# Order of VectorE's work in a graph kernel's projection stage: products and scores two steps back, the dense rows' inverse and shift among the spread rows

## The reference

```python
Q = jnp.einsum('nf,hfd->hnd', x, qw)
K = jnp.einsum('nf,hfd->hnd', x, kw)
Qr = Q[:, row]
alpha = jnp.einsum('hed,hed->he', Qr, K[:, col]) / scale
seg_max = jax.vmap(lambda a: jax.ops.segment_max(a, col, num_segments=n))(alpha)
a = jnp.exp(alpha - seg_max[:, col])
...
h = (h - mu) / jnp.sqrt(var + EPS) * ln_gamma + ln_beta
h = h * jax.nn.sigmoid(h)
return h @ out_w + out_b
```

## Time and profile before

| | us |
|---|---|
| three timed runs, median (lowest to highest) | 3175.5 (3161.36 to 3175.55) |
| the profiled execution | 3167.55 |
| its span, from first to last instruction | 3165.4 |
| busy in the span: DVE | 2318.9 (73%) |
| busy: ACT | 2112.9 (67%) |
| busy: POOL | 1909.8 (60%) |
| busy: PE | 1851.7 (58%) |
| mean share of the DMA queues q1 and q0 | 50.8% and 17.0% |

### The profile page before, as it was taken

How to read it: one execution, slowest core, us unless ns; L and a number is a source line. 1 busy time by engine, 2 the same in 40 slices (tenths; PEclk the granted TensorE clock), 3 DMA queues, 4 the chain that set the end, 5 groups by cost and what they waited for, 6 DMA issues and landing times.

```text
span 3165.4 us, 54101 instructions
## 1 busy us (share of the span) xinstructions
PE 1851.7 (58%) x9516; PEld 1390.9 (44%) x9516; DVE 2318.9 (73%) x8807; ACT 2112.9 (67%) x5382; POOL 1909.8 (60%) x1839
## 2 busy tenths in 40 slices
PE   4666666444555453777777666657656666344442
PEld 4566565333333332445554333346545555233332
DVE  7888878766666664777886666658868888788883
ACT  4888887434444333878887788845547777499995
POOL 6777775788888885333332755457757555045554
PEclk9777877677777776989898898889987777655555
DMA  5889987333333335999998899968867777344441
GB/s 185 298 291 299 303 294 249 70 62 64 61 60 61 61 54 144 336 340 331 337 353 303 306 322 322 323 198 257 264 202 264 254 254 254 119 131 135 126 133 53
DMA packets 325460, 670.59 MB, mean 212 GB/s; under 512 B 56604, under 2 KB 116127, under 8 KB 325396
## 3 DMA queue, kind: packets, MB, share of 16 engines
q1 hardware_dynamic: 244980, 554.40, 50.8%
q0 software_dynamic: 80416, 115.57, 17.0%
HBM read 346.98 MB, written 326.96 MB: 213 GB/s over the span
## 4 chain that ended last, share of the span: by engine, by line
DVE 17%; ACT 14%; issue 10%; DMA 9%; PE 7%; DVEq 2%; POOL 1%; ACTq 1%; SPq 0%; POOLq 0%
ACT node_out L1145 8%; DMA node_in<-y_nodes 4%; DVE acc L1512 3%; DMA node_in<-x_table 3%; PE ps L982 2%; DMA acc_dump<-acc 2%; ACT new_rows L1145 2%; DVE n_stats L1459 2%; DVE e_stats L1459 2%; PE ps L993 1%; DVE node_in L1763 1%; DVE pre L1865 1%; DVE pre L1932 1%; DVE a_stats L1459 1%; ACT gate L1321 1%
## 5 line engine op out<-in xcount | busy, mean ns | idle before, releaser
L1145 ACT ACTIVATE node_out<-node_in,n_shift,n_root 128x128 f32<-128x128 f32 (+1 forms) x1176 | 468.0, 482 | 125.1 <-DVE n_shift L1476 124.5
L702 POOL DMA_INDIRECT sums<-gat_sums,dst_safe_i x200 | 189.4, 947 | 306.0 <-DVE pre L1763 240.6
L767 POOL DMA_INDIRECT gat_sums<-sums,add_idx x200 | 328.9, 1644 | 68.0 <-issue 60.0
L819 POOL DMA_INDIRECT out_dram<-new_rows,out_index x200 | 200.2, 1001 | 251.1 <-ACT new_rows L1145 200.1
L1459 DVE BATCH_NORM_STATS2 n_stats<-node_in 128x6 f32<-128x256 f32 (+1 forms) x784 | 279.3, 419 | 75.1 <-DMA node_in<-y_nodes 61.8
L710 POOL DMA_INDIRECT src_rows<-x_table,row_i x208 | 204.5, 983 | 151.0 <-issue 52.3
L710 POOL DMA_INDIRECT sums<-x_table,row_i x192 | 189.7, 988 | 121.7 <-issue 47.2
L702 POOL DMA_INDIRECT own_rows<-x_table,row_i x200 | 195.9, 980 | 67.1 <-issue 55.5
L702 POOL DMA_INDIRECT src_rows<-in_x_dram,src_i x200 | 193.9, 970 | 69.4 <-issue 60.1
L710 POOL DMA_INDIRECT own_rows<-in_x_dram,dst_safe_i x200 | 195.2, 976 | 61.0 <-issue 59.8
L1154 ACT ACTIVATE t_a<-ps 128x512 f32<-128x512 f32 (+1 forms) x202 | 118.6, 587 | 164.6 <-PE ps L862 164.3
(11 more groups left out here) (346 smaller groups left out, 6594.1 us busy)
## 6 DMA issues: line engine op xcount, KB each, us to landing
own_rows<-x_table SPq DMA_DIRECT2D x300, 256.0 KB, 3.0
x_table<-node_out SPq DMA_DIRECT2D x144, 512.0 KB
acc_dump<-acc SPq DMA_DIRECT2D x200, 264.0 KB
node_in<-x_table SPq DMA_DIRECT2D x96, 512.0 KB
x_table<-new_rows SPq DMA_DIRECT2D x150, 256.0 KB
gat_sums<-node_x2t SPq DMA_DIRECT2D x49, 528.0 KB, 5.9
node_sums<-gat_sums SPq DMA_DIRECT2D x48, 528.0 KB
node_in<-in_x_dram SPq DMA_DIRECT2D x48, 512.0 KB
```

Of the source, the lines that this page charges most:

```text
L702: g_.indirect_dma_start(out=to[:, g.b, j, 0:width], out_offset=None, in_=tab, in_offset=bass.IndirectOffsetOnAxis(ap=indices(j), axis=0)). ...
L767: g_.indirect_dma_start(out=gat_sums[:, :], out_offset=bass.IndirectOffsetOnAxis(ap=add_idx[:, g.b, j:j + 1], axis=0), in_=sums[:, g.b, j, ...
L819: g_.indirect_dma_start(out=out[:, :], out_offset=bass.IndirectOffsetOnAxis(ap=at_tile(out_index, g, j), axis=0), in_=new_rows[:, g.b, j, ...
L1145: last = sc.activation(to[0:pn, g.b, j, :], rows[0:pn, g.b, j, 0:F], ACT.Identity, bias=NORM[k][2][0:pn, g.b, j:j + 1], scale=root[0:pn, j ...
```

## The change

In this stage's call of `pipeline` on DVE, products and score sums go from a lag of one step to two and stand between and behind the last spread rows. The inverse and the shift, so far one function between the second and the third spread row, are two functions now, one behind the first and one behind the second spread row. The addition of the constant row and the statistics of the dense block, so far ahead of the products, come last in the step.

```diff
                 v.tensor_tensor(node_in[0:pn, g.b, :, :], node_in[0:pn, g.b, :, :],
                                 local3_bc[0:pn, None, :].to_broadcast([pn, DJ, F]), ALU.add).then_inc(D["n_pre"].sem, 1)
+
+            def nodes_x3_moments(g):
+                pn = dense_p(g)
                 wait_done(dve, D["n_pre"], g)
                 wait_free(dve, D["n_row"], g)
                 moments((D, "n", g, node_in, pn, DJ))
 
-            pipeline(dve, DENSE_FULL, edges(spread[0], spread[1]) + [nodes(1, shifts(D, "n"))] + edges(spread[2], spread[3])
-                     + [nodes(0, nodes_x3_more)] + edges((1, products), (1, score_sums)))
+            def node_inverses(g):
+                at = NORM["n"][1][0:dense_p(g), g.b, :]
+                wait_done(dve, D["n_rt"], g)
+                v.reciprocal(at, at).then_inc(D["n_rc"].sem, 1)
+
+            def node_shifts(g):
+                pn = dense_p(g)
+                wait_done(dve, D["n_rc"], g)
+                shift_of(D, "n", g, pn, DJ, NORM["n"][1][0:pn, g.b, :])
+
+            pipeline(dve, DENSE_FULL, edges(spread[0]) + [nodes(1, node_inverses)] + edges(spread[1]) + [nodes(1, node_shifts)]
+                     + edges(spread[2], (2, products), spread[3], (2, score_sums)) + [nodes(0, nodes_x3_more), nodes(0, nodes_x3_moments)])
             dve.wait_ge(L["score"].sem, L["score"].at(STEPS))
```

## The result

The changed kernel took 3128.69 us, the median of 4 runs (3123.94 to 3132.63), beside 3174.49 us for the kernel before, the median of 4 runs (3161.36 to 3175.55). The ratio is 0.9864, with a 95% interval of 0.9835 to 0.9894: 45.8 us less. The prediction was 3125 us, in a range of 3104 to 3155.

What follows compares the result with a forecast made beforehand. A ring of waits between DVE and ACT bound the 7.22 us step; afterwards DVE's queue would, at 6.25 us. Saving 43 us in the loop plus 3 outside, 46, gave 3121.5 to 3129.5, so 3125 us, range 3104 to 3155.

Steps and rivals of the forecast that it cites:

- ring through `gate`: DVE and ACT before the change: node_out, copies, products, sums, spread rows, inverse, shift, node_out, 7.23 us round.
- DVE's queue, 6.03 us: DVE's instructions in one step, start to start, sum to 6.03 us; with the branch about 6.2, the largest bound.
- four terms that had no row of their own: Gaps in DVE's sum chosen between two ends: spread row to products, products to spread row, spread row to sums, variance to spread row.
- The branch, 0.15 to 0.18 us a step: DVE's loop branch, once in two steps: half of 0.36 us of bare register work between products and sums.
- Dependent spread rows: On DVE a dependent spread row starts after 0.50 us, an independent instruction after 0.27; two bare pairs a step before.
- ACT's ring, 5.98 us: From node_out 5.00 us to the next root, then inverse, spread row, shift and node_out: 5.98 us a step.
- Rival 4: On DVE, sums and products hide all register steps; ACT binds at 5.9 to 6.0 us, saving 54 to 60; chance 0.08.
- The loads' ring: Dense block loads over two steps: 7.55 us plus L, issue to landing; at most 6.05 a step with L 4.56.
- Rival 1: Dense block loads bind: landing in 5.3 to 6.1 us, steps of 6.4 to 6.8, 19 to 38 saved; chance 0.22.
- Rivals 2 and 3: DVE's inverse waits for ACT's root, 14 us slower, chance 0.04; register steps fill DVE, 0 to 15 saved, chance 0.08.
- The signs: Stage profile: products every 6.0 to 6.4 us, no `gate` wait, shorter `n_shift` wait, inverse within 0.3, DVE above 0.9.
- The sum: Stage saving: 0.97 us in each of 44 loop steps, 43 us, plus 3 us in written-out steps, 46 us.

Runs made afterwards that it cites:

- e2: Kernel before with inverse and shift set between spread rows, products and sums last at a lag of one step; 3155.56 us, ratio 0.9961.
- e1: Kernel before with its order kept and only products and score sums put back to a lag of two steps; 3151.73 us, ratio 0.9944.
- e3: Changed kernel with the dense sums ahead of products and score sums, lag two and mixed order kept; 3151.49 us, ratio 0.993 to the kernel before.
- e8: Changed kernel with the second spread row directly behind the first, ahead of inverse and shift; 3127.7 us in one run, mean step 6.56 us.
- e4: Changed kernel with inverse and shift both behind the first spread row, the other spread rows set apart by products and sums; 3124.53 us, ratio 0.9854.
- e7: Changed kernel storing only one row of eight of each finished dense block; 3125.5 us in one run, step 6.33 us.
- e6: Changed kernel with dense sums ahead of products and one row of eight of each finished dense block stored; 3136.77 us in one run.

## Why the prediction was right

*The rings.* The prediction read the step of before as a ring through `gate`. `e2` leaves that ring closed with inverse and shift in their new places, and stays at 7.0 us; the wait is there, and the ring's legs add up to 6.98. `e1` opens it and leaves the order, and the step falls to 6.9, nearly all of it DVE's queue with its gaps. The third part is needed too: with lag and mixed order but the dense sums ahead of the products (`e3`) the step is still 6.89. The prediction named this place in the change and gave it no term.

*DVE's queue, 6.03 us.* Measured 6.07 to 6.08 in the step without a branch. Of the four terms that had no row of their own, spread row to products was taken as 0.35 and is 0.28, products to spread row 0.60 and is 0.61, spread row to sums 0.35 and is 0.26, and variance to spread row 0.30 and is 0.46. That these errors cancel is luck; the 0.04 to 0.05 that are left come from inverse and shift to the spread rows behind them, 0.23 each where 0.21 was taken.

*The branch, 0.15 to 0.18 us a step.* This is the term that was mis-sized, and it was read at the wrong place. The prediction took it from products to sums, 1.11 us, but that is a row of the step without a branch. The branch stood between sums and spread row and lay bare for 0.26 us a pass, 0.13 a step, so the term came near its size by luck. In the changed kernel the two kinds of step are 0.49 us apart, 0.24 a step: 0.40 a pass at the branch, which now stands behind a variance of 0.17 us instead of sums of 0.69 and lies bare, and 0.07 between the last spread row and the sums, whose reason is open. The regular step is 6.32 us where 6.25 was forecast; 0.07 us over 44 steps are 3 us.

*Dependent spread rows.* 0.23 us for each pair set apart, and `e8` puts it back for one pair: 0.22. The prediction set against this the sentence of the Trainium skill's page "VectorE: DVE Perf Modes", section "The DRAIN you can't avoid", that the next operation does not start until the pipe is empty. The same section goes on that a next operation that is not held starts earlier, which the prediction left out; the traces agree with that: an independent instruction starts 0.27 us after a spread row of 0.35 us, one that waits for the row's semaphore after 0.50.

*ACT's ring, 5.98 us.* Measured 6.04: 5.01 to the root and 1.03 from the root to `node_out`. It lies just beneath DVE's queue; `e4` shortens it and gains nothing, so ACT's ring does not bind. Rival 4 did not come, since the register work is not hidden.

*The loads' ring.* Its form was right, 7.55 + L for two steps; with 4.4 us for L it is 12.0, and by the rows after up to 12.5. It was just short of binding. The prediction's last leg left out the branch, which lies between the addition and `node_out` of every second step: 4.75 us there and 4.34 in the other, where 4.18 was added up. That the ring would bind if products and sums stood between the addition and `node_out` was not said, and is what `e3` cost. Rival 1 itself came only in single steps, worth about 3 us by `e7`. Of the rule in the Trainium skill's page "DMA: Bandwidth & Descriptors", section "Latency and other measured facts", that the access time of HBM grows with load, little is seen in these loads: a median of 4.17 us at 196 GB/s and 4.24 at 270 (`e6`, `e3`), 4.14 in the kernel before and 4.37 in the changed kernel at 292 GB/s. What makes single `own_rows` loads take 6.5 us is not settled; the long steps that they made went with the stores' traffic, in one run.

*Rivals 2 and 3.* Past the first two steps, where it waited 4.16 and 1.55 us, the inverse waited no microsecond for a root in the changed kernel, and the step fell. Neither was seen.

*The signs.* The wait for `gate` is gone and ACT's wait for `n_shift` is 1.1 us, as said. Two signs missed: DVE's busy share is 0.89 from 2460 to 2560 us where above 0.9 was expected, and in the step with the branch the inverse starts 0.58 us after the root's end instead of within 0.3. Half of the regular steps, those of 6.56 us, lie outside the 6.0 to 6.4 that was named; their mean does not.

*The sum.* 46 us were predicted for the stage, and between the two profiled executions it is 40.6 us shorter: 3 us are missing by the regular step, 3 by the late loads. The medians of the whole kernel stand 45.8 us apart. That this meets the 46 so closely is luck: the runs of the kernel before lie 14 us apart and those of the changed kernel 9.

## What to carry to other kernels

Write out every ring that a step takes part in, those over two steps too, with each leg from a row, and compare their sums with the longest queue. After a change the next ring can be just beneath: here 6.32 us for DVE's queue, 6.0 for ACT, about 6.25 for the loads, so that a queue shorter by a further 0.25 us brought nothing. Work that doesn't belong to a ring should stand outside it: the dense sums last, with products and sums ahead of the addition, were worth 0.54 us a step with the same instructions. Two short dependent instructions belong apart with an independent one between them. The loop's branch belongs behind a long instruction: the step that holds it was 0.29 us longer with the branch behind sums of 0.69 us (`e1`) and 0.49 behind a variance of 0.17. Look for the branch itself in the trace before you price it; the prediction priced another gap.

## What was not expected of the hardware

With the branch of a loop on DVE behind an instruction of 0.17 us, the step that holds it was 0.49 us longer, 0.40 of it at the branch. A loop body of four steps halved its number and gave 0.08 us a step (6.35 to 6.27).

A load of a dense block took nearly the same time with a quarter less traffic in the queues: a median of 4.17 us at 196 GB/s against 4.24 at 270. Its size did matter: with an eighth of the block it landed after 1.9 us, and the wait of 1.4 us in every second step was gone.

One chip ran the kernel before in 3510 us and another in 3167 to 3170. The ratio of one kernel order was the same on both, 0.9862 and 0.9869.
